# Plain attention's scores: from one product of three bf16 parts on 96 rows to two float32r parts on two row groups of 64

## The chip, the cores and the metric

One core of a Trainium2 chip runs the whole kernel. The metric is the device time of one execution in microseconds. TensorE (PE) multiplies matrices; its weight loads stand as PEld in the profile. VectorE is DVE, ScalarE is ACT, GpSimd is POOL, and SyncE (SP) issues all DMAs of the passes told of here, in order, on one queue.

## What is computed

128 images go through an embedding, a plain attention of 12 heads without an output projection, a causal attention, a mixture of 64 small experts and a final norm. The part that the change touches:

```
tokens = patches @ W_map.T + b_map + positions        # 197 tokens of 192 numbers
x      = layernorm(tokens) * ln_w + ln_b
q, k, v = per head of 16: x_h @ Wq.T + bq, ...        # 12 heads
att    = softmax(q @ k.T / sqrt(16))
tokens = tokens + att @ v                             # plain attention
```

The causal attention follows, with its own q, k and v.

## The kernel before

The program is a chain of passes, each over all 128 images: `embed_pass`, `attend_pass` (plain), `attend_pass` (causal), routing and experts, combination. In each pass every engine runs its own list of steps in order, written out by hand: step c works on several images at once, each in another phase (b2 = c - 2, b3 = c - 3 and so on), and semaphores order the engines. Four places in SBUF rotate (R = 4). Tokens are padded to 198 = 2 x 99.

**Embedding.** TensorE makes tokens, q, k and v in f32. ScalarE writes the high bf16 part of q and k (`split_high`, L310), VectorE the rest (`left_of`, L338), GpSimd the middle and the low part (L282, L284). SyncE stores the three parts in `scr["qk1"]` (L263): 96 partitions x 12 pieces of 396 bytes an image.

**Plain attention.** A score is a sum over 16 numbers of a head, each split in three bf16 parts; the six products of parts that count are stacked on 96 rows (`STACK`), so a score tile is one bf16 product over 96 rows, 99 columns of weights and 198 columns streamed. Each image's scores are made twice. First as *query scores* (L821, queries on partitions): VectorE takes each query's maximum (L770), TensorE turns the maxima (L925), ScalarE copies them negated (L721), GpSimd splits them in three parts (`max_parts`, L611 to L618), and SyncE writes these as three rows under the stack of q (L561), where rows of ones stand under k. Two images later they are made as *key scores* (L843, keys on partitions, 99 rows, maximum already taken off), and ScalarE takes the exponential (L713).

Step c has six slots k = 0 to 5. In each, TensorE first makes four key scores of image b4 (`key_scores`, L826; two PSUM buffers of two banks each, `sk`), then four query scores of image b2 as two fills f = 2k and 2k + 1 (`query_scores`, L808; two banks, `sq`: fill f waits until VectorE has taken the maxima of fill f - 2). After that come other products by slot:

- k = 0: transposes of image b6 (L916), then value products of b5 (L858)
- k = 1: the turned maxima of b3 (L925), which wait for VectorE's L775, then turned sums (L864)
- k = 2: q of the next attention for b6 (`turned_times`, L873, twelve float32r products), then value products
- k = 3: turned sums
- k = 4: k of the next attention (L873), then value products
- k = 5: v of the next attention (`tokens_times`, L881)

ScalarE's order in a step is the exponential of each slot, then in slot 0 the cast of the transposed image (L716), in slot 2 the high part of q (L179), in slot 5 the copy of v (L739), with copies of sums between. VectorE's order is the two maxima of each slot, then in slot 0 the low part of the cast (L775), in slots 1 and 3 the division by the sums (L791, L793), in slot 2 the rest of q (L784). SyncE's order in a step: six loads of q and k (L552), the three writes of maxima once GpSimd has made them (wait at L559), the load of tokens (L567), the stores (L578, L581).

Of the kernel before, what the change touches and what calls it, by code (L numbers as in the profile page):

```python
# [30 lines left out]
HEADS = 12  # L31
# [150 lines left out]
def embed_pass(nc, n, A, scr):  # L182
    R = 4
    DEPTH = 4
    with ExitStack() as ctx:
# [17 lines left out]
        rest = m.sb("e_rest", [CH, 2, 2, 2, SP])  # L203
        parts = m.sb("e_parts", [CH, R, 2, 2, PARTS, SP], BF16)
# [30 lines left out]
        middle = m.event("e_middle", 2)  # L235
        low = m.event("e_low", 2)
# [5 lines left out]
        def _(sp):  # L242
# [10 lines left out]
            def step(c):  # L253
# [4 lines left out]
                if b.inside(n):  # L258
                    sp.wait_ge(v_copied.sem, v_copied.at(b))
                    for rows in SHARES:  # L260
                        sp.dma_start(scr["tv1"][b.number, rows], tv[rows, b.place]).then_inc(stored.of(b), 16)
                    sp.wait_ge(low.sem, low.at(b))
                    sp.dma_start(scr["qk1"][b.number].rearrange("i c a p s -> p (i c a) s"),  # L263
                                 parts[:, b.place].rearrange("p i c a s -> p (i c a) s")).then_inc(stored.of(b), 16)
# [3 lines left out]

        @block.gpsimd
        def _(pool):  # L270
            for e in (middle, low):
                e.seed(pool)

            def step(c):
                b = c - 3
                u = b.parity
                if b.inside(n):
                    for i in range(2):
                        pool.wait_ge(left.sem, left.at(b, i + 1))
                        pool.wait_ge(stored.of(b - 4), stored.at(b - 4))  # L280
                        m.hold(pool)
                        pool.tensor_copy(parts[:, b.place, i, :, place_of(i, 1)], rest[:, u, i]).then_inc(middle.sem, 1)  # L282
                        pool.wait_ge(middle.sem, middle.at(b, i + 1))
                        pool.tensor_tensor(parts[:, b.place, i, :, place_of(i, 2)], rest[:, u, i], parts[:, b.place, i, :, place_of(i, 1)],  # L284
                                           ALU.subtract).then_inc(low.sem, 1)
            pipeline(pool, n, DEPTH, R, step)

        @block.scalar
        def _(act):
# [5 lines left out]
            def step(c):  # L295
# [11 lines left out]
                for i, (done, p) in enumerate(((q_done, qp), (k_done, kp))):  # L307
                    if b3.inside(n):
                        act.wait_ge(done.sem, done.at(b3))
                        split_high(nc.scalar, parts[:, b3.place, i, :, place_of(i, 0)], p[:], SCALES[i]).then_inc(high.sem, 1)  # L310
# [9 lines left out]
        def _(dve):  # L320
# [14 lines left out]
            def left_of(b3, i, p):  # L335
                dve.wait_ge(high.sem, high.at(b3, i + 1))
                dve.wait_ge(low.sem, low.at(b3 - 2, i + 1))
                nc.vector.scalar_tensor_tensor(out=rest[:, b3.parity, i], in0=p[:], scalar=SCALES[i],  # L338
# [89 lines left out]
def attend_pass(nc, n, A, scr, causal):  # L428
# [4 lines left out]
    with ExitStack() as ctx:  # L433
# [97 lines left out]
        def heads_of(fill):  # L531
            return fill // 6, 2 * (fill % 6)
# [266 lines left out]
        def _(pe):  # L799
# [84 lines left out]
            def step(c):  # L884
# [7 lines left out]
                for k in range(6):  # L892
# [5 lines left out]
                    if b4.inside(n):  # L898
                        key_scores(b4, k)
# [750 lines left out]
```

## Time and profile before

| | us |
|---|---|
| median of 3 runs | 4905.67 |
| lowest and highest | 4903.66, 4913.21 |
| the profiled execution | 4908.6 |
| its span (first to last instruction) | 4906.8 |

The page gives the busy time of each engine and the span in 40 slices. Plain attention lies between 905 and 2468 us of the span, embedding before it, causal attention from 2474 to 3856 us.

```profile
## 2 busy tenths in 40 slices
PE   8999999899999999999979999999999788889964
...
DVE  4555555566666666666556666666666599960057
ACT  3444444466666666666635555555555377764446
POOL 3444444466666666666656666666666488861135
PEclk9999999899999999999979999999999699999965
```

Each digit is a tenth of a slice of 122.7 us; slices 8 to 20 are plain attention. A busy TensorE is not one at its peak: the record of a product lasts from its start to its result, and products follow each other at shorter distances than their records are long, so distances between starts are what counts.

### The profile page before, as it was taken

The numbers are of one execution on the slowest core, as the hardware profiler recorded it, in microseconds if no ns is written. First come the engines' busy times: TensorE is split into PE (matmuls) and PEld (weight loads), VectorE is DVE, ScalarE is ACT, GpSimd is POOL, SyncE is SP. The second block draws the span as 40 slices with busy tenths as digits, with TensorE's granted clock in tenths as the row PEclk, the third lists the DMA queues.
The fourth block names the chain that finished last, engine by engine and source line by source line (L and its number), as shares of the span: only waits on it lengthen the run. The fifth ranks groups of instructions, "written<-read, shape, count | busy, mean of one in ns | idle before, by whom it ended". The sixth has DMA issues, their size and how long they took to land. (4 is left out here: it accounts for less than half of the span.)

```text
span 4906.8 us, 161306 instructions
## 1 busy us (share of the span) xinstructions
PE 4504.7 (92%) x48311; PEld 3888.5 (79%) x48311; DVE 3050.0 (62%) x8728; ACT 2746.9 (56%) x6788; POOL 2724.9 (56%) x4491
## 2 busy tenths in 40 slices
PE   8999999899999999999979999999999788889964
PEld 8999999688888888888867777777777566669953
DVE  4555555566666666666556666666666599960057
ACT  3444444466666666666635555555555377764446
POOL 3444444466666666666656666666666488861135
PEclk9999999899999999999979999999999699999965
DMA  6777777677777777777656665665666133339978
GB/s 172 202 201 201 202 202 203 145 168 168 168 164 169 167 166 167 168 167 164 149 122 131 134 132 131 132 134 130 130 135 132 56 94 92 93 104 276 276 237 255
DMA packets 697918, 789.88 MB, mean 161 GB/s; under 512 B 367345, under 2 KB 519887, under 8 KB 697840
## 3 DMA queue, kind: packets, MB, share of 16 engines
q1 hardware_dynamic: 697840, 788.92, 66.1%
q8 instruction: 40, 0.66, 0.1%
q14 instruction: 38, 0.31, 0.0%
HBM read 519.30 MB, written 265.72 MB: 160 GB/s over the span
## 5 line engine op out<-in xcount | busy, mean ns | idle before, releaser
L770 DVE TENSOR_REDUCE a_mx<-a_sq 99x2 f32<-99x394 f32 x1536 | 798.4, 561 | 377.2 <-PE a_sq L821 376.9
L770 DVE TENSOR_REDUCE c_mx<-c_sq 99x2 f32<-99x198 f32 (+1 forms) x1536 | 642.3, 459 | 315.0 <-PE c_sq L821 314.7
L713 ACT ACTIVATE a_ex<-a_sk 99x792 f32<-99x792 f32 (+1 forms) x768 | 638.8, 832 | 106.6 <-PE a_sk L843 56.6
L713 ACT ACTIVATE c_ex<-c_sk 99x792 f32<-99x792 f32 (+1 forms) x768 | 512.3, 667 | 247.1 <-PE c_sk L837 173.9
L379 PE MATMUL e_tokp<-e_wmap,e_ptT 128*99 128x192 f32 x3072 | 544.3, 327 | 20.8 <-DVE e_cvar L332 20.8
L634 POOL TENSOR_SCALAR_AFFINE_SELECT c_ex<-c_ex 99x396 f32<-99x396 f32 (+1 forms) x768 | 422.0, 550 | 232.2 <-ACT c_ex L713 228.1
L379 PEld LDWEIGHTS e_tokp<-e_wmap,e_ptT 128*99 128x99 f32 x3072 | 483.2, 167 | 21.3 <-issue 20.8
L821 PE MATMUL a_sq<-a_ks,a_qs 96*99 96x198 bf16 x3072 | 441.5, 255 | 31.3 <-DMA a_ks<-scr_qk 16.4
L282 POOL CAST e_parts<-e_rest 96x396 bf16<-96x396 f32 x256 | 176.8, 691 | 483.1 <-DVE e_rest L338 483.1
L821 PE MATMUL c_sq<-c_ks,c_qs 96*99 96x99 bf16 (+1 forms) x3072 | 417.7, 231 | 0.0
L843 PE MATMUL a_sk<-a_qs,a_ks 99*99 99x198 bf16 (+1 forms) x3072 | 408.5, 254 | 3.0 <-issue 2.2
L818 PE MATMUL c_sq<-c_maskb,c_identb 99*99 99x198 bf16 x1536 | 376.7, 262 | 21.3 <-DMA c_ks<-scr_qk 17.9
L843 PEld LDWEIGHTS a_sk<-a_qs,a_ks 99*99 99x99 bf16 (+1 forms) x3072 | 287.4, 126 | 124.6 <-issue 112.9
L821 PEld LDWEIGHTS a_sq<-a_ks,a_qs 96*99 96x99 bf16 x3072 | 293.2, 126 | 82.3 <-DVE a_mx L770 46.8
L858 PE MATMUL a_pvp<-a_ex,a_vx 99*32 99x198 f32 (+1 forms) x6144 | 337.9, 337 | 0.6 <-issue 0.5
L821 PEld LDWEIGHTS c_sq<-c_ks,c_qs 96*99 96x99 bf16 x3072 | 325.1, 128 | 0.0
L858 PE MATMUL c_pvp<-c_ex,c_vx 99*32 99x198 f32 (+1 forms) x6144 | 278.1, 299 | 27.5 <-issue 0.8
L698 ACT COPY c_ot<-c_pvp 128x198 f32<-128x198 f32 x384 | 124.7, 325 | 299.7 <-PE c_pvp L858 299.7
L858 PEld LDWEIGHTS c_pvp<-c_ex,c_vx 99*32 99x32 f32 (+1 forms) x6144 | 163.1, 110 | 131.8 <-DVE c_on L793 76.9
L284 POOL TENSOR_TENSOR e_parts<-e_rest,e_parts 96x396 bf16<-96x396 f32 x256 | 224.5, 877 | 20.5
L818 PEld LDWEIGHTS c_sq<-c_maskb,c_identb 99*99 99x99 bf16 x1536 | 194.5, 127 | 51.8 <-DVE c_mx L770 31.6
L843 PE MATMUL c_sk<-c_qs,c_ks 99*99 99x198 bf16 x1536 | 213.4, 261 | 9.6 <-issue 8.8
(196 smaller groups left out, 11487.7 us busy)
## 6 DMA issues: line engine op xcount, KB each, us to landing
e_ptT<-in_x SPq DMA_DIRECT2D x128, 594.0 KB
x_w<-in_fc SPq DMA_DIRECT2D x128, 576.0 KB, 5.8
scr_qk<-e_parts SPq DMA_DIRECT2D x128, 445.5 KB
scr_qk<-a_parts SPq DMA_DIRECT2D x128, 445.5 KB
scr_tv<-e_tv SPq DMA_DIRECT2D x128, 288.0 KB
a_tv<-scr_tv SPq DMA_DIRECT2D x128, 288.0 KB
scr_tv<-a_res SPq DMA_DIRECT2D x128, 288.0 KB
c_tv<-scr_tv SPq DMA_DIRECT2D x128, 288.0 KB
```

The lines of the kernel that those rows point to most:

```text
L282: pool.tensor_copy(parts[:, b.place, i, :, place_of(i, 1)], rest[:, u, i]).then_inc(middle.sem, 1)
L284: pool.tensor_tensor(parts[:, b.place, i, :, place_of(i, 2)], rest[:, u, i], parts[:, b.place, i, :, place_of(i, 1)], ALU.subtract).then_i ...
L379: mm = nc.tensor.matmul(tokp[b.parity][:, t], ptT[:, b.place, k, t * TT:(t + 1) * TT], wmap[:, k], start=(k == 0), stop=(k == KC - 1))
L634: pool.affine_select(block_of, block_of, pattern=[[0, G], [1, TT]], compare_op=ALU.is_ge, fill=0.0, base=0, channel_multiplier=-1).then_in ...
L698: nc.scalar.copy(ot[:, b.parity, g], pv).then_inc(o_copied.sem, 1)
L713: nc.scalar.activation(to, of, ACT.Exp).then_inc(exped.sem, 1)
L770: nc.vector.reduce_max(mx[:, b2.parity, qt, h:h + 2], sq[f % 2][:, :, 0:width], AX.X).then_inc(maxed.sem, 1)
L818: nc.tensor.matmul(bank[:, :, qt * TT:(qt + 1) * TT], identb[:], maskb[:].broadcast_to([TT, 2, TT]), start=True, stop=False, skip_group_ch ...
L821: mm = nc.tensor.matmul(bank[:, j, 0:keys], qs[0:STACK, b.place, h + j, qt * TT:(qt + 1) * TT], ks[0:STACK, b.place, h + j, 0:keys], start ...
L843: mm = nc.tensor.matmul(buf[0:rows, a, j * SP:(j + 1) * SP], ks[:, b.place, h, kt * TT:kt * TT + rows], qs[:, b.place, h, :], start=True, ...
L858: mm = nc.tensor.matmul(to, vx[0:rows, b.place, kt, G * g + j, :], of, start=(kt == 0), stop=(kt == 1), skip_group_check=causal)
```

## The change

- **Embedding** keeps two float32r parts of q and k (high and rest) instead of three bf16 parts. VectorE writes the rest straight into the parts; GpSimd has no work left in this pass. The store has 96 x 8 pieces of 792 bytes.
- **Layout in plain attention.** The three products of parts that count take 48 rows of f32r. Heads 0 to 5 stand on partitions 0 to 47, heads 6 to 11 on 64 to 111, and the maxima, now two parts, on the two rows after each. Loads are eight instead of six for an image (the same bytes, pieces of 4752 instead of 2376 bytes), writes of maxima four instead of three; GpSimd has two operations instead of four for them.
- **Scores.** `shared_scores` issues key scores of image b4 by turns with query scores of image b2; the order of the query fills is such that the two always lie on different row groups of 64. They are float32r products over 48 or 50 rows, 99 columns of weights, 198 streamed.
- **Start.** Rows of ones are set over 32 partitions by GpSimd (first in its list) and over 32 by VectorE, and SyncE's first load waits for both.
- The causal pass has its bf16 scores as before, and its parts are still three bf16 parts.

```diff
-        rest = m.sb("e_rest", [CH, 2, 2, 2, SP])
-        parts = m.sb("e_parts", [CH, R, 2, 2, PARTS, SP], BF16)
+        parts = m.sb("e_parts", [CH, R, 2, 2, 2, SP], F32R)
...
-                    sp.wait_ge(low.sem, low.at(b))
+                    sp.wait_ge(left.sem, left.at(b))
                     sp.dma_start(scr["qk1"][b.number].rearrange("i c a p s -> p (i c a) s"),
-                                 parts[:, b.place].rearrange("p i c a s -> p (i c a) s")).then_inc(stored.of(b), 16)
+                                 parts[:, b.place].rearrange("p i c a s -> p (i c a) s").bitcast(F32)).then_inc(stored.of(b), 16)
...
-        @block.gpsimd
-        def _(pool):
-            for e in (middle, low):
-                e.seed(pool)
-
...
-                if b.inside(n):
-                    for i in range(2):
-                        pool.wait_ge(left.sem, left.at(b, i + 1))
-                        pool.wait_ge(stored.of(b - 4), stored.at(b - 4))
-                        m.hold(pool)
-                        pool.tensor_copy(parts[:, b.place, i, :, place_of(i, 1)], rest[:, u, i]).then_inc(middle.sem, 1)
-                        pool.wait_ge(middle.sem, middle.at(b, i + 1))
-                        pool.tensor_tensor(parts[:, b.place, i, :, place_of(i, 2)], rest[:, u, i], parts[:, b.place, i, :, place_of(i, 1)],
-                                           ALU.subtract).then_inc(low.sem, 1)
-            pipeline(pool, n, DEPTH, R, step)
...
             def left_of(b3, i, p):
                 dve.wait_ge(high.sem, high.at(b3, i + 1))
-                dve.wait_ge(low.sem, low.at(b3 - 2, i + 1))
-                nc.vector.scalar_tensor_tensor(out=rest[:, b3.parity, i], in0=p[:], scalar=SCALES[i],
-                                               in1=parts[:, b3.place, i, :, place_of(i, 0)], op0=ALU.mult,
+                dve.wait_ge(stored.of(b3 - 4), stored.at(b3 - 4))
+                nc.vector.scalar_tensor_tensor(out=parts[:, b3.place, i, :, 1], in0=p[:], scalar=SCALES[i],
+                                               in1=parts[:, b3.place, i, :, 0].bitcast(F32), op0=ALU.mult,
                                                op1=ALU.subtract).then_inc(left.sem, 1)
...
-        qs = m.sb(X + "qs", [AUG, R, HEADS, SP], BF16)
-        ks = m.sb(X + "ks", [AUG, R, HEADS, SP], BF16)
+        if causal:
+            qs = m.sb(X + "qs", [AUG, R, HEADS, SP], BF16)
+            ks = m.sb(X + "ks", [AUG, R, HEADS, SP], BF16)
+        else:
+
+            qs = m.sb(X + "qs", [128, R, HC, SP], F32R)
+            ks = m.sb(X + "ks", [128, R, HC, SP], F32R)
...
-        mxp = m.sb(X + "mxp", [HEADS, 2, PARTS, SP], BF16)
+        mxp = m.sb(X + "mxp", [HEADS, 2, PARTS, SP], BF16) if causal else m.sb(X + "mxp", [HEADS, 2, 2, SP], F32R)
...
-        max_in_place = m.transfers(X + "max_in_place", 3)
+        max_in_place = m.transfers(X + "max_in_place", 3 if causal else 4)
...
+        def half(h):
+            return slice(64 * (h // HC), 64 * (h // HC) + 3 * DH), slice(64 * (h // HC), 64 * (h // HC) + 3 * DH + 2)
+            if not causal:
+
+                return ((0, 6), (1, 6), (0, 8), (1, 8), (0, 10), (0, 0), (1, 10), (1, 0), (0, 2), (1, 2), (0, 4), (1, 4))[fill]
...
+                    else:
+                        if b.is_number(0):
+                            sp.wait_ge(ks_ones, 1)
+                            sp.wait_ge(ks_ones_above, 1)
+                        for c2 in range(2):
+                            for stack, i, at, of in ((qs, 0, 0, slice(0, 1)), (qs, 0, DH, slice(0, 2)),
+                                                     (ks, 1, 0, slice(0, 2)), (ks, 1, 2 * DH, slice(0, 1))):
+                                at += 64 * c2
+                                sp.dma_start(stack[at:at + (of.stop - of.start) * DH, b.place].rearrange("r h s -> r (h s)").bitcast(F32),
+                                             qk_in[b.number, i, c2, of].rearrange("a (d h) s -> (a d) (h s)",
+                                                                                  d=DH)).then_inc(qk_in_place.of(b), 16)
                 if b.is_number(0):
                     sp.dma_start(w[:], A["wout" if causal else "wqkv2"].rearrange("(c p) d -> p c d", p=CH)).then_inc(weighed, 16)
...
+                    else:
+                        for a in range(2):
+                            for c2 in range(2):
+                                at = 64 * c2 + 3 * DH + a
+                                sp.dma_start(qs[at:at + 1, b.place].bitcast(F32),
+                                             mxp[c2 * HC:(c2 + 1) * HC, b.parity, a].bitcast(F32)).then_inc(max_in_place.of(b), 16)
                 b = c - 2
...
+            def ones_of_keys(of):
+                pool.memset(of, ONE_TWICE if causal else 1.0).then_inc(ks_ones, 1)
+                pool.wait_ge(ks_ones, 1)
+            if not causal:
+                ones_of_keys(ks[32:64].rearrange("p r h s -> p (r h s)").bitcast(F32))
...
+                if not causal:
+                    pool.tensor_tensor(low, of, high.bitcast(F32), ALU.subtract).then_inc(max_low.sem, 1)
+                    return
...
-                        act.wait_ge(max_rest.sem, max_rest.at(b3 - 2))
+                        if causal:
+                            act.wait_ge(max_rest.sem, max_rest.at(b3 - 2))
+                        else:
+                            act.wait_ge(max_low.sem, max_low.at(b3 - 2))
...
+            if not causal:
+                nc.vector.memset(ks[96:128].rearrange("p r h s -> p (r h s)").bitcast(F32), 1.0).then_inc(ks_ones_above, 1)
...
+            def shared_scores(b4, b2, k):
+
+                g, kt = k // 2, k % 2
+                rows = TT - kt
+                if b4.inside(n):
+                    bank_of_keys(b4, k)
+                for j in range(G):
+                    f = 2 * k + j // 2
+                    if b4.inside(n):
+                        h = G * g + j
+                        mm = nc.tensor.matmul(sk[k % 2][0:rows, j // 2, (j % 2) * SP:(j % 2 + 1) * SP],
+                                              ks[half(h)[1], b4.place, h % HC, kt * TT:kt * TT + rows],
+                                              qs[half(h)[1], b4.place, h % HC], start=True, stop=True)
+                        if j == G - 1:
+                            mm.then_inc(scored_k.sem, 1)
+                    if b2.inside(n):
+                        qt, h = heads_of(f)
+                        h += j % 2
+                        if j % 2 == 0:
+                            bank_of_queries(b2, f)
+                        mm = nc.tensor.matmul(sq[f % 2][:, j % 2], qs[half(h)[0], b2.place, h % HC, qt * TT:(qt + 1) * TT],
+                                              ks[half(h)[0], b2.place, h % HC], start=True, stop=True)
+                        if j % 2:
+                            mm.then_inc(scored_q.sem, 1)
...
-                    if b4.inside(n):
-                        key_scores(b4, k)
-                    if b2.inside(n):
-                        query_scores(b2, 2 * k)
-                        query_scores(b2, 2 * k + 1)
+                    if causal:
+                        if b4.inside(n):
+                            key_scores(b4, k)
+                        if b2.inside(n):
+                            query_scores(b2, 2 * k)
+                            query_scores(b2, 2 * k + 1)
+                    else:
+                        shared_scores(b4, b2, k)
...
-              "qk1": ([n, 2, 2, PARTS, CH, SP], BF16), "qk2": ([n, 2, 2, PARTS, CH, SP], BF16),
+              "qk1": ([n, 2, 2, 2, CH, SP], F32), "qk2": ([n, 2, 2, PARTS, CH, SP], BF16),
```

## Rows read from the trace of the kernel before

**Rows 1.** Windows: us; busy PE, PEld, DVE, ACT, POOL; PEclk, DMA, GB/s.

```profile
200.00:800.00 600.00, 600.00 (x4430) 596.32 (x4429) 321.10 (x710) 265.20 (x796) 272.90 (x355) 1.00 0.76 202
1200.00:2300.00 1100.00, 1090.81 (x13281) 916.70 (x13279) 756.21 (x1660) 732.36 (x1292) 674.11 (x1106) 1.00 0.74 167
```

**Rows 2.** Timeline, TensorE, one image of plain attention: start us, us, work, count.

```profile
1497.48 0.34 PE L881 MATMUL a_pvp<-a_wh,a_hTl 96*99 96x192 f32 x2
1497.65 0.51 PE L843 MATMUL a_sk<-a_qs,a_ks 99*99 99x198 bf16 x4
1498.00 0.51 PE L821 MATMUL a_sq<-a_ks,a_qs 96*99 96x198 bf16 x4
...
1501.61 0.41 PE L873 MATMUL a_work<-a_hTh,a_wh 96*96 96x198 f32 x2
...
1502.59 0.35 PE L873 MATMUL a_work<-a_hTl,a_wh 96*96 96x198 f32 x2
1502.87 0.88 PE L858 MATMUL a_pvp<-a_ex,a_vx 99*32 99x198 f32 x16
1503.68 0.55 PE L843 MATMUL a_sk<-a_qs,a_ks 99*98 99x198 bf16 x4
...
1505.70 0.41 PE L873 MATMUL a_work<-a_hTh,a_wh 96*96 96x198 f32 x2
...
1509.59 0.51 PE L843 MATMUL a_sk<-a_qs,a_ks 99*99 99x198 bf16 x4
```

**Rows 3.** Timeline, VectorE, the same image; x2 are two maxima.

```profile
1499.63 0.57 DVE L775 TENSOR_TENSOR a_hTl<-a_work,a_hTh 96x396 fp32r<-96x396 f32 x1 [0.21 <-ACT a_hTh L716]
1500.36 1.04 DVE L770 TENSOR_REDUCE a_mx<-a_sq 99x2 f32<-99x394 f32 x2 [0.16 <-PE a_sq L821]
...
1503.66 0.57 DVE L784 SCALAR_TENSOR_TENSOR a_rest<-a_work,a_parts 96x396 f32<-96x396 f32 x1 [0.77 <-ACT a_parts L179]
1504.44 1.04 DVE L770 TENSOR_REDUCE a_mx<-a_sq 99x2 f32<-99x394 f32 x2 [0.22 <-PE a_sq L821]
```

**Rows 4.** Timeline, last pass, half clock: products on partitions 0-63, 64-127 alternating.

```profile
4763.86 1.60 PE L1552 MATMUL o_zp<-o_yb,o_mix 64*99 64x192 f32 x8 [1.87 <-POOL o_yb L1482]
...
4763.97 0.93 PEld L1552 LDWEIGHTS o_zp<-o_yb,o_mix 64*99 64x99 f32 x6
```

**Rows 5.** Timeline, embedding, TensorE: f32 products on all rows.

```profile
400.79 2.12 PE L379 MATMUL e_tokp<-e_wmap,e_ptT 128*99 128x192 f32 x12
402.74 0.84 PE L409 MATMUL e_qp<-e_xT,e_wqkv 97*96 97x198 f32 x4
```

**Rows 6.** Timeline, routing pass, TensorE: from 99 rows to 64 rows.

```profile
4102.62 0.33 PE L1263 MATMUL r_cTp<-r_ident,r_cw 99*64 99x99 f32 x2
4102.88 0.38 PE L1266 MATMUL r_dTp<-r_ident,r_dw 64*99 64x64 f32 x2
```

**Rows 7.** Timeline, ScalarE, the same image of plain attention.

```profile
1497.85 0.48 ACT L739 COPY a_res<-a_pvp 99x384 f32<-99x384 f32 x1 [0.60 <-PE a_pvp L881]
1498.39 0.83 ACT L713 ACTIVATE a_ex<-a_sk 99x792 f32<-99x792 f32 x1
1499.12 0.48 ACT L716 CAST a_hTh<-a_work 96x396 fp32r<-96x396 f32 x1
```

**Rows 8.** Timeline, start of plain attention: SyncE's queue and GpSimd.

```profile
905.48 0.43 SPq L552 DMA_DIRECT2D a_qs<-scr_qk  x1
905.96 0.42 SPq L552 DMA_DIRECT2D a_ks<-scr_qk  x1
...
908.08 4.06 POOL L600 MEMSET a_ks<- 3x4752 f32 x1
```

**Rows 9.** Timeline, plain attention, SyncE's queue (SPq): DMA issues.

```profile
1501.07 0.32 SPq L552 DMA_DIRECT2D a_ks<-scr_qk  x1
1503.59 2.35 SPq L561 DMA_DIRECT2D a_qs<-a_mxp  x3
...
1509.88 1.38 SPq L552 DMA_DIRECT2D a_ks<-scr_qk  x1
```

## What the change will do to the time

> **What bounds the kernel now.** I read the windows first, for the share of each engine inside a pass; then the timelines of TensorE, ScalarE and VectorE for one image of plain attention, for the distances between starts; then the places elsewhere in the trace where two products run on two row groups; last SyncE's queue. In embedding TensorE is busy for all of 600 us, and GpSimd, whose work the change takes away there, for 273 [rows 1]: no other engine sets that pass. In plain attention TensorE is busy 1091 of 1100 us at granted clock 1.00, VectorE 756, ScalarE 732 [rows 1]. But "busy" hides who is late. One image takes 11.94 us: its slot 0 begins at 1497.65, the next one's at 1509.59 [rows 2]. In it TensorE waits twice for VectorE's maxima, before fill 5 and before fill 9: the maxima end at 1501.40 and 1505.48, and the float32r products behind these fills start 0.21 and 0.22 us later [rows 2, 3], which is just two score products. So the period is one loop in three parts:
>
> - A, from slot 0 (1497.65) to the q products (1501.61), 3.96 us: copy of v, exponential, cast (ScalarE), low part and two maxima (VectorE), fill 5.
> - B, to the k products (1505.70), 4.09 us: q products, high part, rest, two maxima, fill 9.
> - C, to the next slot 0, 3.89 us: TensorE alone.
>
> A faster score counts only where it shortens one of these.
>
> **Embedding.** It loses GpSimd's casts and subtractions, and its store gets 768 pieces of 792 bytes instead of 1152 of 396. TensorE's list is the same and is full [rows 1]: 0 us. The new wait of VectorE (L338, for the store of four images before) is one that ScalarE's high part in front of it already has; behind it on VectorE queue the reciprocal and the normalization, and TensorE's transposes wait for those. The store now waits for VectorE, earlier than for GpSimd. If TensorE stopped covering this pass, VectorE at 321 us of 600 is next, so nothing is lost there.
>
> **The scores.** An image has 48 score products of 0.088 us (four in 0.35 us [rows 2]), 4.2 us of TensorE. Afterwards they are 24 pairs. The price of a pair is nowhere in this pass, so I bound it. If both products run side by side, it is that of one float32r product of 198 columns: eleven distances from 1501.61 to 1502.69 (the second of the two at 1502.59), 0.093 us with the start [rows 2]. If one follows the other it is 0.175 (two bf16 distances) to 0.186 us. The nearest row is the last pass, where f32 products alternate between partitions 0-63 and 64-127: eight within 1.60 us, the last record 0.52 long, so eight starts in 1.08 us at half clock, that is about three intervals of 0.32 to 0.43 between pairs [rows 4]. One such product alone with the whole array takes 0.163 us at full clock (twelve in 1.95 us [rows 5]), 0.325 at half. A pair thus costs what one costs, weight loads included: six of these end within 0.93 us [rows 4]. I take 0.093 us.
>
> **Switching the array's division.** Going from 99 rows to 64 rows, the next product starts at 4102.88, where the distance of its predecessors (0.085) would give 4102.79: 0.09 us more [rows 6]. The value products on groups of columns show the same: 1502.87 instead of 1502.78 [rows 2]. Before, only value products switch, in and out, three times an image. Afterwards every change between scores and other products is a switch: nine more (in and out of slots 0 to 5, less those that value products already pay), 0.84 us of TensorE an image. TensorE's own account is then -4.2 + 2.2 + 0.8 = -1.2 us. Not all of it arrives, by the loop:
>
> - A. The copy of v starts 0.03 us after its products, now 0.11 after slot 0 begins instead of 0.20, for slot 0 starts one switch later. Then 0.54 to the exponential, 0.73 to the cast, 0.51 to the low part [rows 3, 7]. The key scores are there in time (3 x 0.093 + 0.25 + 0.04 = 0.57 before 0.65). The low part begins at 1.89; a maximum can follow 0.48 after it, as one does another (1.04 less 0.56 [rows 3]). Before, it came after 0.73, because fill 2 was late (the bracket "PE a_sq" in [rows 3]); fill 2 now comes about 0.3 us earlier. Two maxima of 1.04: 3.41. Then 0.21 - 0.175 + 0.186 + 0.09 for fill 5 and a switch: **3.72** instead of 3.96.
> - B. The rest of q starts 2.05 us after the q products [rows 2, 3], unchanged. The maxima follow after 0.48 instead of 0.78 (again they waited for TensorE), 1.04, and 0.32 for fill 9 and a switch: **3.89** instead of 4.09. Fill 6 must be done 2.53 us after the q products began: 1.26 to the value products, 0.81 through them [rows 2], 0.38 for the scores, 2.45. That is close; a dearer pair would show here.
> - C. Slot 5's eight scores shrink from 0.70 to 0.37, two switches add 0.18: **3.74** instead of 3.89.
>
> The sum is 11.35 us, 0.59 less than 11.94; 128 images give -75.5 us. What is late next is VectorE's and ScalarE's part of A and B.
>
> **The maxima's split.** GpSimd has two operations less, and the three writes become four; they land for a step that begins over 5 us later. Cover: that distance. Cost 0 while SyncE keeps up (below).
>
> **The start.** SyncE's first load was issued at 905.48, before the ones were set; the memset takes 4.06 us [rows 8], set by its length of 4752, which stays. Now the load waits for it: +3.7 us; and an image needs two more issues of 0.48 us [rows 8]: +1.0. All loads are queued behind this wait, and TensorE waits for them. Its bounds are 0 (a faster memset) and 6 us. I take +4.7.
>
> **Sum.** -75.5 + 4.7 = -70.8 us. Against the profiled execution, 4908.6 (1.8 over its span), that is 4837.8; the median of the runs is 2.9 lower, so 4835. About 0.2% (10 us) is what a measurement can tell from no change. The forecast's own range is 4800 to 4880: below, switches that cost half and gaps between engines that close further; above, pairs of 0.11 us (eight pairs lie on the loop) and SyncE just over the loop.
>
> **Rival 1, slower: the two products don't run side by side.** Then a pair costs 0.175 to 0.186 us and the switches are paid for nothing. Key scores would end 0.25 to 0.3 us later than the copy of v allows, and fills 5 and 9 and slot 5 have eight more pairs at +0.08 to +0.093: the loop is 12.26 to 12.39, +0.32 to +0.45 an image, and with the start 4951 to 4968. It decides from about 0.14 us a pair. Against it stand the pairs in [rows 4]; for it, that those were f32 at half clock, where a product is streamed long enough to hide any weight load: nothing shows two float32r weight loads of 99 columns within 0.093 us. Chance 0.17.
>
> The Trainium skill says in "TensorE: Matmul & The Clock Gate", section "Part 3: Packing small matmuls — row/col tiling", that weight loads overlap products in flight only where the row group differs. By that rule each group would load and multiply by turns, and the time would be this rival's. The pairs in [rows 4] follow each other at the pace of one product with loads between, so this trace speaks against it.
>
> **Rival 2: issue is the limit.** With 48 products in half the time TensorE's sequencer may not keep up. The densest stretch now is sixteen value products whose starts lie within 0.55 us (0.88 less a record of 0.33 [rows 2]), 0.037 us each; a pair needs 0.046 each. So it should hold. If it didn't, with a pair of 0.124, the loop would be 11.67 and the time 4876. Chance 0.06.
>
> The same page, section "Part 2: What happens when you issue a matmul", gives about 62 ns of microcode per product where hardware decoding is off. That would be this rival; the sixteen value products above are faster than it.
>
> **Rival 3: SyncE's queue becomes the loop.** SyncE waits from 1501.39 to 1503.59 for the split maxima [rows 9]: 2.2 of 11.94 us, so it is occupied for 9.74. Two more loads (0.48 each) and one more write (2.35 / 3 = 0.78) make 11.48, already over 11.35. Against: one load is stalled for 1.38 us instead of 0.43 behind the big store [rows 9], and with half as many pieces to queue this stall may go (10.5). For: if each of the first ones stalls so, it is 12.4. At 11.6 the time is 4867, and from 11.9 on nothing is gained. Chance 0.12.
>
> **Rival 4: the clock.** Plain attention has granted clock 1.00; the last pass, with long idle stretches, ran its row-group products at 0.50, the level of 1.2 GHz [rows 4]. If plain attention fell to that level, TensorE's part of the loop would double: over 500 us slower. TensorE stays busy most of the time, so 0.03. That the change leaves score time as it is for another reason: 0.02, near 4900 to 4940.
>
> **How the numbers follow.** Forecast 0.60, rivals 0.17, 0.06, 0.12, 0.03, 0.02. Faster by over 0.2%: the forecast, rival 2 and most of rival 3, 0.74; within 0.2%: 0.06; slower 0.20. The range reaches from 4800 into rival 1, to 4960.
>
> **What the profile will show.** Right: in plain attention a key score and a query score start under 0.02 us apart and pairs 0.09 to 0.10; about 0.09 extra at each change to other products; about 11.35 us an image; TensorE waits for VectorE longer than now before fills 5 and 9; embedding's length as before; the first load about 4 us later. Wrong: pairs at 0.14 or more (rival 1), SyncE without a wait at L559 (rival 3), a clock below 1.00 in that pass (rival 4), or an image over 11.7 us.

## The result, and the profile after

The changed kernel takes 5876.1 us (median of four, 5856.82 to 6111.58; the highest ran at a granted clock of 0.71 and is left out of the ratio). The kernel before, run beside it, takes 4909.44 (4903.66 to 4924.45). The ratio is 1.195, interval 1.189 to 1.202: nearly a fifth slower, where 4835 was forecast and 4800 to 4960 given as range. The profiled execution is 5856.82 us, its span 5854.7.

The page of the changed kernel, TensorE's busy share and granted clock in 40 slices:

```profile
PE   8999998999999999999999979999999978888975
PEclk9999995555555555555555579999999988999985
```

From the seventh slice to the 23rd the clock is at half; from the eighth on TensorE is busy for 90% of each slice or more. The windows of the changed kernel, with the columns of [rows 1]:

```profile
200.00:800.00 600.00, 600.00 (x4432) 596.33 (x4431) 272.67 (x710) 264.31 (x797) 0.00 (x0) 1.00 0.78 224
1200.00:2300.00 1100.00, 1100.00 (x8165) 812.64 (x8165) 480.92 (x1019) 458.09 (x794) 368.28 (x567) 0.50 0.44 103
3500.00:4500.00 1000.00, 909.68 (x12601) 756.87 (x12599) 656.96 (x1719) 531.45 (x1052) 614.39 (x1145) 1.00 0.61 132
```

Embedding's window is as full as before, with GpSimd at 0.00 [rows 1]; causal attention (the third row) runs at 1.00. Plain attention, from 901 to 3417 us instead of 905 to 2468, holds the whole loss: 2516 us for 1563. The granted clock falls at 897.65 us, in TensorE's wait for the pass's first loads, and stays at 0.50, the level of 1.2 GHz (1.00 is 2.4 GHz), for 2505 us. Before, it was there from 889.4 to 933.8 us only.

The timeline of TensorE in the changed kernel, one image at half clock; it answers to [rows 2]:

```profile
2001.33 0.48 PE L883 MATMUL a_sk<-a_qs,a_ks 50*99 50x198 f32 x1
2001.33 0.48 PE L893 MATMUL a_sq<-a_ks,a_qs 48*99 48x198 f32 x1
2001.61 0.37 PE L883 MATMUL a_sk<-a_qs,a_ks 50*99 50x198 f32 x1
2001.61 0.37 PE L893 MATMUL a_sq<-a_ks,a_qs 48*99 48x198 f32 x1
2001.78 0.37 PE L883 MATMUL a_sk<-a_qs,a_ks 50*99 50x198 f32 x1
2001.78 0.37 PE L893 MATMUL a_sq<-a_ks,a_qs 48*99 48x198 f32 x1
...
2020.74 0.48 PE L883 MATMUL a_sk<-a_qs,a_ks 50*99 50x198 f32 x1
```

A key score and a query score start together, and pairs follow each other by 0.17 us: 198 columns at 1.2 GHz are 0.165. So the change does what it says, and the pair has the price that the forecast gave it, at half the clock. Slot 0 comes again after 19.41 us instead of 11.94. TensorE sets this period alone: VectorE, which it waited for before [rows 2, 3], now waits for it:

```profile
2002.03 1.04 DVE L793 TENSOR_REDUCE a_mx<-a_sq 99x2 f32<-99x394 f32 x2 [2.12 <-PE a_sq L893]
2005.24 1.04 DVE L793 TENSOR_REDUCE a_mx<-a_sq 99x2 f32<-99x394 f32 x2 [0.98 <-PE a_sq L893]
```

The kernel before came out of its own half-clock start here (timeline, TensorE, kernel before):

```profile
914.52 1.04 PE L821 MATMUL a_sq<-a_ks,a_qs 96*99 96x198 bf16 x4 [0.33 <-DVE a_mx L770]
...
929.82 0.87 PE L843 MATMUL a_sk<-a_qs,a_ks 99*99 99x198 bf16 x4 [1.91 <-issue]
930.48 0.87 PE L821 MATMUL a_sq<-a_ks,a_qs 96*99 96x198 bf16 x4
931.14 0.87 PE L843 MATMUL a_sk<-a_qs,a_ks 99*98 99x198 bf16 x4
931.80 0.92 PE L821 MATMUL a_sq<-a_ks,a_qs 96*99 96x198 bf16 x4
```

Rounds (a round is what TensorE does in one step) of query scores alone, four at a time with gaps, did not raise it; the first scores of keys and queries without a gap, on 96 and 99 rows, did, at 933.8. These are the products that the change puts on 64 rows.

### The profile page after: what moved, and what is told of

It reads as the page before. It is cut to its first block and busy times, and to the rows that moved or that the text cites. A ratio compares the mean times of both kernels' runs of the same rounds, so it can differ in the third digit from the quotient of the medians.

```text
span 5854.7 us, 160403 instructions
## 1 busy us (share of the span) xinstructions
PE 5465.2 (93%) x48311; PEld 4447.1 (76%) x48311; DVE 3023.2 (52%) x8729; ACT 2761.3 (47%) x6788; POOL 2222.7 (38%) x3723
## 5 line engine op out<-in xcount | busy, mean ns | idle before, releaser
L883 PEld LDWEIGHTS a_sk<-a_qs,a_ks 50*99 50x99 f32 (+1 forms) x3072 | 566.0, 273 | 328.1 <-issue 292.0
L893 PE MATMUL a_sq<-a_ks,a_qs 48*99 48x198 f32 x3072 | 756.2, 397 | 23.5 <-DMA a_ks<-scr_qk 19.8
L883 PE MATMUL a_sk<-a_qs,a_ks 50*99 50x198 f32 (+1 forms) x3072 | 754.4, 395 | 1.1 <-issue 1.1
L908 PE MATMUL a_pvp<-a_ex,a_vx 99*32 99x198 f32 (+1 forms) x6144 | 595.0, 537 | 0.0
L893 PEld LDWEIGHTS a_sq<-a_ks,a_qs 48*99 48x99 f32 x3072 | 566.0, 273 | 28.3 <-issue 20.4
L626 POOL CAST a_mxp<-a_mxn 12x198 fp32r<-12x198 f32 x128 | 43.4, 339 | 977.4 <-ACT a_mxn L742 977.4
L848 PE MATMUL c_sq<-c_maskb,c_identb 99*99 99x198 bf16 x1536 | 377.1, 263 | 21.1 <-DMA c_ks<-scr_qk 17.6
L908 PEld LDWEIGHTS a_pvp<-a_ex,a_vx 99*32 99x32 f32 (+1 forms) x6144 | 228.5, 158 | 181.4 <-issue 78.4
L923 PE MATMUL a_work<-a_hTh,a_wh 96*96 96x198 f32 x1024 | 301.1, 396 | 3.1 <-DVE a_rest L807 1.9
L716 ACT COPY a_ot<-a_pvp 128x198 f32<-128x198 f32 x384 | 124.4, 324 | 376.8 <-PE a_pvp L908 376.8
L923 PE MATMUL a_work<-a_hTl,a_wh 96*96 96x198 f32 x1024 | 272.3, 367 | 0.0
```

Of the source, the lines that this page charges most:

```text
L626: pool.tensor_copy(high, of).then_inc(max_high.sem, 1)
L716: nc.scalar.copy(ot[:, b.parity, g], pv).then_inc(o_copied.sem, 1)
L848: nc.tensor.matmul(bank[:, :, qt * TT:(qt + 1) * TT], identb[:], maskb[:].broadcast_to([TT, 2, TT]), start=True, stop=False, skip_group_ch ...
L883: mm = nc.tensor.matmul(sk[k % 2][0:rows, j // 2, (j % 2) * SP:(j % 2 + 1) * SP], ks[half(h)[1], b4.place, h % HC, kt * TT:kt * TT + rows] ...
L893: mm = nc.tensor.matmul(sq[f % 2][:, j % 2], qs[half(h)[0], b2.place, h % HC, qt * TT:(qt + 1) * TT], ks[half(h)[0], b2.place, h % HC], st ...
L908: mm = nc.tensor.matmul(to, vx[0:rows, b.place, kt, G * g + j, :], of, start=(kt == 0), stop=(kt == 1), skip_group_check=causal)
```

## The experiments

Four theories stood at the start. H: the pass only starts at half clock, and once up the clock stays. P: pairs leave TensorE too little to stream. R: products that read a row group of 64, half the array, don't raise the clock (as it was put for the first run, they don't keep it up either). F: float32r scores as such, or another edit, keep it down. All runs but the last are one execution with a profile, beside one of the kernel before on the same chip (4904.18 for the first three runs told here; 4907.85 for those on one row group, on all rows, of the kernel before on 48 rows, and with products at the start of the pass; 4907.2 for the other four). Such single times of the kernel before spread from 4898 to 4925 us, so a difference of a few us between two runs shows nothing.

**Raise the clock once.** The added products, 24 of 512 columns on all 128 rows, stand ahead of the first value products of image 6 (`fill` is a tile of ones):

```
+                        if not causal and b6.is_number(0):
+                            for _ in range(24):
+                                nc.tensor.matmul(pvp[:], fill[:, 0:128], fill[:, 128:640], start=True, stop=True)
                         value_products(b5, 2)
```

> The changed kernel with 24 bf16 products of 512 columns on all 128 rows, written to a bank that is free, once at the seventh step of plain attention. Theory H (the pass only starts cold, because its first products are few; once the clock is up it stays): granted clock 1.00 from the burst on, 11.35 us an image, 4840 to 4860 us. Theory R (products on row groups of 64 don't keep the clock up): it rises with the burst and falls back within some tens of us, or doesn't rise; about 19.4 us an image, 5860 to 5890 us.

Measured: 4900.88 us, against 4904.18 for the kernel before. TensorE's timeline of this kernel, round the added products (L1005):

```profile
959.08 6.44 PE L1005 MATMUL a_pvp<-a_fill 128*128 128x512 bf16 x24
```

And the window of plain attention:

```profile
1200.00:2300.00 1100.00, 1083.07 (x13475) 820.74 (x13477) 755.52 (x1684) 750.26 (x1311) 611.33 (x936) 1.00 0.78 170
```

The first five follow each other by 0.427 us, those from the seventh on by 0.216; the clock is 1.00 from 961.3 to 2456 us, without a break, with no product added after them. So H is right as to staying up: the same rounds that ran at 0.50 for 2505 us keep 1.00, and the half of R that says that products on 64 rows can't keep the clock up falls. An image takes 11.76 us, not the 11.35 of the forecast. (The kernel before has such products in its routing pass, with a result that nobody reads.)

**One added product in each slot**, ahead of the scores, 512 columns on all 128 rows:

```
+                        if b4.inside(n) and b2.inside(n):
+                            bank_of_keys(b4, k)
+                            nc.tensor.matmul(sk[k % 2][:, 0, 0:512], fill[:, 0:TT], fill[:, 128:640], start=True, stop=True)
                         shared_scores(b4, b2, k)
```

> The changed kernel with one bf16 product of 512 columns on all 128 rows ahead of the scores in each of the six slots of every step of plain attention; it is overwritten by the key scores. Theories H and R: the clock rises to 1.00 and stays; 12.2 to 12.6 us an image (11.35, plus the part of 6 x 0.22 and three switches that lies on the loop), 4940 to 5000 us. If neither holds (the clock is down for another reason than what TensorE does): 0.50 throughout, about 22 us an image, 6190 us.

Measured: 5313.91 us. The image takes 22.47 us at 0.50 until 1617.6 us; there the clock rises, and to the pass's end it is 1.00, with an image of 12.94 us. Neither forecast held. Six such products, apart from each other, raise it late, after some 30 images that look alike; why in that one stays open. Once up it held here too.

**Alternation undone**: four key scores, then four query scores in each slot.

```
                 for j in range(G):
                     if b4.inside(n):
                         ... key score
+                for j in range(G):
                     if b2.inside(n):
                         ... query score
```

> The changed kernel with the alternation undone: in each slot four key scores, then four query scores, on the same row groups and with the same data, so that no two products run side by side except where the groups change. Theory R: the clock stays at 0.50, because half the rows work at a time; about 19.4 + 24 x 0.167 = 23.4 us an image, 6370 us. A theory P (it is the pairs: 24 instead of 48 stretches of streaming leave TensorE with too little work) expects clock 1.00, about 12.4 us an image and 4965 us.

Measured: 5857.77 us, clock 0.50 throughout, image 19.47 us against 19.41. TensorE's timeline of this kernel:

```profile
2001.89 0.48 PE L882 MATMUL a_sk<-a_qs,a_ks 50*99 50x198 f32 x1
2001.90 0.48 PE L894 MATMUL a_sq<-a_ks,a_qs 48*99 48x198 f32 x1
```

The list holds four products of one kind and then four of the other, and yet they run side by side, the later ones taken forward onto the idle row group. So this run, which was meant to tell P from R, could not. The order by turns is worth 0.06 us an image, and it has no part in the clock.

**P against R: all scores on one row group**, so one after the other (heads 6 to 11 read the rows of heads 0 to 5):

```
         def half(h):
-            return slice(64 * (h // HC), 64 * (h // HC) + 3 * DH), slice(64 * (h // HC), 64 * (h // HC) + 3 * DH + 2)
+            return slice(0, 3 * DH), slice(0, 3 * DH + 2)
```

> Changes the computation: all twelve heads read rows 0-49 (heads 0 to 5 twice), so every score product runs on the one row group 0-63 and the products follow one another; their count, type, columns and rows are as in the changed kernel. Question: why does the granted clock stay at 0.50 in plain attention. Theory P (pairs: two products at a time leave too little streaming): the serial scores stream twice as long, as before the change, so the clock rises soon after the pass's start and stays up; image 12.2 to 12.5 us (48 products at 0.093 and the switches), 4940 to 4980 us. Theory R (products on 64 rows, half the array, don't raise the clock, however long they stream): 0.50 through the pass; 24 more products of 0.167 us at half clock, image about 23.4 us, 6350 to 6400 us.

Measured: 6402.26 us; image 23.41 us. The window of plain attention in this kernel:

```profile
1200.00:2300.00 1100.00, 1100.00 (x6772) 861.69 (x6768) 429.35 (x846) 382.38 (x658) 306.71 (x470) 0.50 0.37 85
```

The scores stream as long as before the change, one after the other, TensorE is busy for all of 1100 us, and the clock is 0.50. P falls: without pairs it stays down as well.

**F against R: the same float32r scores on the whole row range**, `half` giving rows 0 to 111 (0 to 113 with the maxima, which are multiplied by zero), with zeros in the unused rows:

```
-            return slice(64 * (h // HC), 64 * (h // HC) + 3 * DH), slice(64 * (h // HC), 64 * (h // HC) + 3 * DH + 2)
+            return slice(0, 112), slice(0, 114)
```

> Changes the computation: each score product reads rows 0-111 (key scores 0-113), that is two heads at once, and the maxima are multiplied by zero; so float32r scores on the whole row range, one after the other, with no row groups and no switches around them. Theory R: the clock rises within some tens of us, as in the kernel before; 48 products of 0.093 us against 0.088 before, image 11.9 to 12.2 us, 4905 to 4945 us (the second memset at the start adds up to 4). Theory P gives the same. Theory F (float32r scores as such, or another edit, keep it down): 0.50 through the pass, over 6000 us.

Measured: 4938.99 us. The clock rises at 943.7, 6 us after key scores and query scores begin to come close behind each other, and stays. Window and two scores from this kernel's views:

```profile
1200.00:2300.00 1100.00, 1100.00 (x12976) 952.37 (x12974) 736.36 (x1622) 721.35 (x1262) 590.39 (x900) 1.00 0.77 164
```

```profile
1501.32 0.26 PE L886 MATMUL a_sk<-a_qs,a_ks 114*98 114x198 f32 x1
1501.41 0.26 PE L896 MATMUL a_sq<-a_ks,a_qs 112*99 112x198 f32 x1
```

F falls: float32r scores of the same columns and count do raise the clock when they read 112 rows. They follow each other at 0.09 to 0.10 us, and the image is 12.21.

**R without the change: the kernel before, its scores cut to rows 0 to 47**, in bf16, one after the other, nothing else touched:

```
-                    mm = nc.tensor.matmul(bank[:, j, 0:keys], qs[0:STACK, b.place, h + j, qt * TT:(qt + 1) * TT],
-                                          ks[0:STACK, b.place, h + j, 0:keys], start=not causal, stop=True,
+                    mm = nc.tensor.matmul(bank[:, j, 0:keys], qs[0:STACK if causal else 48, b.place, h + j, qt * TT:(qt + 1) * TT],
+                                          ks[0:STACK if causal else 48, b.place, h + j, 0:keys], start=not causal, stop=True,
...
-                                                  ks[:, b.place, h, kt * TT:kt * TT + rows], qs[:, b.place, h, :],
+                                                  ks[0:AUG if causal else 48, b.place, h, kt * TT:kt * TT + rows], qs[0:AUG if causal else 48, b.place, h, :],
```

> The kernel before the change, with its bf16 score products cut to rows 0-47, so the sums over the other rows and the maxima are left out of the scores; all else as before. Serial, bf16, one row group. Theory R: the clock stays at 0.50 in plain attention although nothing else of the change is there; image 23 us or more, over 6200 us. Theories P and F: the clock rises at about 930 to 960 us as before; nine more switches an image, 4905 to 5010 us.

Measured: 6281.47 us. The kernel before, with nothing of the change but fewer rows, stays at 0.50 from 890 us to the end of the pass, with an image of 22.81 us; its window:

```profile
1200.00:2300.00 1100.00, 1100.00 (x6949) 833.07 (x6948) 412.47 (x866) 397.45 (x675) 356.26 (x580) 0.50 0.39 87
```

**R at the rise itself: the 24 products on 64 rows.** One change to the first run:

```
-                                nc.tensor.matmul(pvp[:], fill[:, 0:128], fill[:, 128:640], start=True, stop=True)
+                                nc.tensor.matmul(pvp[:], fill[0:64, 0:128], fill[0:64, 128:640], start=True, stop=True)
```

> The run with 24 products of 512 columns in image 6, with one thing changed: the 24 products read 64 rows instead of 128; they are as many, as long and as dense. Theory R (products on 64 rows don't raise the clock): it stays at 0.50 in and after them, and the pass runs as in the changed kernel, plus at most 24 x 0.427 = 10 us: 5860 to 5875 us. If any dense stream raises it: about 4901 us, as with 128 rows.

Measured: 5869.29 us. TensorE's timeline and two windows of this kernel, to be read beside the first run's:

```profile
957.37 10.42 PE L1005 MATMUL a_pvp<-a_fill 64*128 64x512 bf16 x24
```

```profile
957.00:967.80 10.80, 10.80 (x31) 3.57 (x33) 0.78 (x2) 0.80 (x2) 0.00 (x0) 0.50 0.37 71
1200.00:2300.00 1100.00, 1100.00 (x8163) 813.13 (x8162) 482.89 (x1024) 459.17 (x794) 370.66 (x568) 0.50 0.45 103
```

As many products, of as many columns, as dense; 128 rows raise the clock 2.2 us after their start, 64 rows don't in 10.4.

**What holds it: one row group, with the 24 products on 128 rows** (the edits of the first run and of the run on one group together).

> Changes the computation: all heads read rows 0-49, so all score products are on one row group, one after the other, and 24 products of 512 columns on 128 rows stand in image 6 to raise the clock. Question: what holds it once it is up. If only the rise needs the whole array and any busy TensorE holds it, it stays at 1.00: image 12.2 of the run on all rows plus nine switches of 0.09 to 0.17 us, 13.0 to 13.8 us, 5060 to 5160 us. If serial 64-row products also lose it, while pairs side by side kept it in the run with pairs: back to 0.50 after the 24 products, image 23.4, 6380 to 6410 us.

Measured: 5134.27 us, clock 1.00 from 968.1 to 2661 us; image 13.35. The window:

```profile
1200.00:2300.00 1100.00, 1100.00 (x11863) 888.93 (x11864) 678.77 (x1484) 658.97 (x1154) 538.15 (x824) 1.00 0.72 149
```

To hold the clock asks less than to raise it: the rounds with serial scores on 64 rows, which could not raise it, keep it. The first run, with pairs, has 11.76 us an image and this one 13.35, so at full clock pairs are worth 1.6 us against the same products one after the other.

**Raise it at the start of the pass**: 40 of these products as TensorE's first work there, while it waits for the loads.

```
+            if not causal:
+                pe.wait_ge(fill_ready, 1)
+                for _ in range(40):
+                    nc.tensor.matmul(pvp[:], fill[:, 0:128], fill[:, 128:640], start=True, stop=True)
             pe.wait_ge(const, n_const)
```

> The changed kernel with 40 products of 512 columns on all 128 rows, of ones, that TensorE does first thing in the pass, into a bank that isn't used yet, while it waits for the first loads (901 to 913 us); nothing else is changed. Theory H (only the cold start is the fault; up once, the clock stays): it rises in these products, stays up from the first image, and the pass loses the 60 us at half clock that the run with 24 products in image 6 had: 4860 to 4885 us. If the thin first images let it fall again, it stays at 0.50 to the end: 5860.

Measured: 5850.0 us. The windows of this kernel show the rise and the fall:

```profile
901.00:904.00 3.00, 2.55 (x7) 0.92 (x8) 1.96 (x2) 0.00 (x0) 3.00 (x1) 0.50 0.07 22
905.00:914.00 9.00, 7.12 (x35) 3.23 (x34) 1.36 (x1) 0.00 (x0) 2.85 (x2) 1.00 0.71 146
915.00:931.00 16.00, 12.80 (x46) 8.45 (x45) 12.78 (x24) 1.61 (x2) 1.44 (x3) 0.50 0.73 128
935.00:950.00 15.00, 14.67 (x132) 9.16 (x131) 8.22 (x17) 7.42 (x14) 2.31 (x5) 0.50 0.55 106
```

It rises at 904.7 and falls at 915.0: the products end at 911.9, TensorE then waits 1.9 us, and the first images have query scores only, four at a time with waits for VectorE between. From 935 on TensorE is busy again, and nothing raises it. So H lacked a condition: a clock raised ahead of these first rounds was lost in them.

**Fewer products**: 8 instead of 24 in image 6.

> The changed kernel with 8 products of 512 columns on 128 rows in image 6 instead of 24. With 24 the granted clock was up from the sixth on. Theory H/R: eight raise it too and save 16 x 0.216 = 3.5 us: 4894 to 4900 us. If the rise needs the whole stretch, it stays or falls back: 5860.

Measured: 4896.97 us against 4907.2; up at 959.6.

**Two places**: 10 products at the start of image 4's round, 8 in image 6's.

> Ten products of 512 columns on 128 rows at the start of image 4's round, where TensorE waits about 1.3 us for the maxima to land, and eight in image 6's. If the clock comes up at 934 to 936 us instead of 961 and the rounds of images 4 and 5 keep it: two rounds of 11.4 and 13 us become 9.5, less 2 us for the products: 4885 to 4893 us. If these thin rounds let it fall, the eight raise it again: 4896 to 4902.

Measured: 4901.47 us. Up at 936.8, down at 940.2, up again at 964.1: the round of image 4 did not keep it either, though TensorE was busy for 2.98 of these 3.42 us. What let the clock fall there was not tried further, and of the ten products no gain is seen.

**The kernel with 8 products, timed in five rounds.**

> The kernel with 8 products in image 6 once more, timed against the kernel before in five rounds, for an interval. By its image of 11.73 us against 11.93 over 122 images (-24 us), and a slower start (rounds of 11.4 and 15.6 us where the kernel before had 9.1 and 9.8: +8 us, and 4.7 for the loads that wait, of which embedding's earlier end gives some back): 4895 to 4900 against 4905 to 4909, ratio 0.997 to 0.999. If the clock's rise hangs on chance, some executions are near 5860.

Measured: 4892.59 us (median of 9, 4891.11 to 4897.82) against 4908.6 (4898.45 to 4918.41): ratio 0.9972, interval 0.9962 to 0.9983. No execution missed the rise, and this version is faster than the kernel before, by 0.3%. The traces give the change only a part of that. Plain attention is 1557.1 us in it, 1562.6 in the kernel before, 5.5 us less. From one product of turned maxima to the next, an image has 11.76 us instead of 11.93, which over 124 images is -21.1; the two rounds ahead of these, here still at half clock and the second with the 8 products in it, have 11.43 and 16.24 us where there were 9.10 and 9.77, +8.8; the start, with the later loads, takes 5.4 us longer and the end 1.4. Embedding is 3.7 us shorter, and causal attention, which the change doesn't touch, 5.4; in the traces of this case that pass has any length from 1371.7 to 1385.1.

## Why the prediction was wrong, step by step

**The step that failed is rival 4.** It named the right event, with a lower bound of its size (over 500 us; it was 947.9 of span, as TensorE at half clock sets the whole loop of 19.41 us), and gave it 0.03, on the ground that TensorE stays busy most of the time. That ground is wrong twice. Busy is not what tells: at 0.50 TensorE was busy 1100 of 1100 us, more than the 1091 at 1.00 [rows 1]. And the mean over the pass says nothing of its beginning. [rows 1] showed that the pass held 1.00; what had raised it, at 933.8 us, the prediction never looked at, though the profile showed the half-clock start of 44.4 us, and there it would have seen that the products that raised it are those that the change halves in rows. In its place the runs showed that the pass starts at 0.50, that scores on 64 rows don't raise the clock from there (nor do 24 dense products on 64 rows), and that one stretch of products on 128 rows ahead of full rounds does. [rows 4] was read for the pairs' distance alone; that these row-group products ran at half clock was put down to the idle stretches of that pass. Whether the products on 64 rows had a part in it there, no run here shows.

The Trainium skill, "TensorE: Matmul & The Clock Gate", section "Part 1: The HAM clock gate (the "warmup" mystery)", lets the gate go by how busy TensorE has been. For the rise, these traces agree only where the scores read 96 rows or more, or where products on 128 rows were added: with scores on 64 rows alone TensorE was busy for 1100 of 1100 us and the clock stayed at 0.50. By that rule rival 4 would have had no chance.

**Rival 1, pairs one after the other: fell.** The pair costs one product, 0.17 us at half clock and 0.09 to 0.10 at full. The rule of the Trainium skill, "TensorE: Matmul & The Clock Gate", section "Part 3: Packing small matmuls — row/col tiling", that a weight load overlaps products in flight only where the row group differs, does not agree with the run on all rows: products of 112 and 114 rows, each with its own weights, follow each other at 0.09 to 0.10 us, where 198 columns at 2.4 GHz are 0.083, and weight loads fill 952 of that window's 1100 us beside them.

**Rival 2, issue: fell.** Two products in 0.09 us are issued without a gap.

**Rival 3, SyncE's queue: fell.** In the run with 24 products SyncE still waits 0.69 us for the split maxima (its load ends at 1509.74, the write starts at 1510.43) and 0.74 ahead of the loads.

**The loop, with the clock up.** Here the forecast's mechanism can be judged, and its size was off too: 11.76 us an image is over the 11.7 that it named as a sign of being wrong. In the timed kernel the means over 110 images are A 3.84, B 4.03, C 3.90 us, where 3.72, 3.89 and 3.74 were forecast and 3.96, 4.09 and 3.89 stood before. The mis-sized term is the switch. TensorE, ScalarE and VectorE in the run with 24 products, one image (three views):

```profile
1505.68 0.33 PE L886 MATMUL a_sk<-a_qs,a_ks 50*99 50x198 f32 x1
...
1509.60 0.42 PE L926 MATMUL a_work<-a_hTh,a_wh 96*96 96x198 f32 x2
...
1513.63 0.43 PE L926 MATMUL a_work<-a_hTh,a_wh 96*96 96x198 f32 x2
...
1515.73 0.33 PE L886 MATMUL a_sk<-a_qs,a_ks 50*98 50x198 f32 x1
...
1515.90 0.26 PE L886 MATMUL a_sk<-a_qs,a_ks 50*98 50x198 f32 x1
...
1515.99 0.25 PE L886 MATMUL a_sk<-a_qs,a_ks 50*98 50x198 f32 x1
...
1516.09 0.25 PE L886 MATMUL a_sk<-a_qs,a_ks 50*98 50x198 f32 x1
...
1516.28 0.42 PE L934 MATMUL a_pvp<-a_wh,a_hTh 96*99 96x192 f32 x2
1516.54 0.34 PE L934 MATMUL a_pvp<-a_wl,a_hTh 96*99 96x192 f32 x2
...
1517.53 0.33 PE L886 MATMUL a_sk<-a_qs,a_ks 50*99 50x198 f32 x1
```

```profile
1506.44 0.83 ACT L733 ACTIVATE a_ex<-a_sk 99x792 f32<-99x792 f32 x1 [0.17 <-PE a_sk L886]
```

```profile
1508.16 1.03 DVE L796 TENSOR_REDUCE a_mx<-a_sq 99x2 f32<-99x394 f32 x2
```

Pairs of one slot start 0.09 to 0.10 us apart, but the second starts 0.17 after the first. The first product after the slot starts 0.19 after the last pair, and the two of 1516.28 take 0.42 where the two after them take 0.34. So a switch costs 0.09 us ahead of the first product, as the prediction read it from [rows 6], and about 0.08 more behind it. [rows 6] held a part of that too, unread: the two products of 64 columns take 0.38 us, those of 99 columns before them 0.33. The two runs whose TensorE is full at 1.00 price it by themselves: an image with 48 serial scores takes 13.35 us where these are on 64 rows and 12.21 where they are on 112; by the reckoning of the prediction the two differ by nine switches, 0.13 us each. On the loop it counts thus: in A the key scores of slot 0 end later and the exponential follows them, not the copy of v; before fills 5 and 9 the products start 0.41 us after the maxima end (1509.60 less 1509.19) instead of 0.31; in C the products of v and the way into slot 0 each pay.

**Embedding at 0, the start at +4.7: nearly right.** Embedding lasts 879.9 us in both traces that have the old one and 874.7 to 878.8 in the twelve that have the new one, so it gave 1 to 5 us where nothing was forecast; TensorE is as full as before, and no run tells where they come from. The first load now follows the pass's first instruction on SyncE by 4.70 us (905.56 less 900.86) instead of 0.43: 4.27 more, where 3.7 was priced for the wait for the ones. That this is near the +4.7 of the whole start is chance: TensorE's first score comes 12.00 us after that instruction instead of 8.27, 3.73 more.

## What to carry to other kernels

Before cutting a product to 64 rows, look in the trace for the stretch that raised TensorE's clock, and ask which of its products would read half the rows afterwards; a pass that starts after a wait may otherwise stay at half clock to its end, with a TensorE that looks full. Where pairs on two row groups pay, a few products over all 128 rows (here eight) brought the clock up, and pairs kept it; ahead of the thin first rounds it was lost again. Price a change of the array's division at both products behind it, not only at the distance to the first.

## What the runs showed of the hardware

- In these kernels the clock's rise went by the rows that products read, not by TensorE's busy time: 0.50 at 1100 of 1100 us busy with scores on 48 to 50 rows in bf16 or float32r, single or in pairs; up at 933.8 and 943.7 us with 96 to 114 rows. In the kernels that stayed at 0.50, too, products on 96 to 128 rows stood between the scores, twelve in a row among them, and did not raise it. The columns of weights were not varied. What the chip counts, and why the run with one product a slot rose at 1617.6 us and not before, stays open.
- Rise and hold are not alike: rounds with scores on one row group of 64, which did not raise the clock in 3022 us of plain attention at 0.50, kept it at 1.00 for 1693 us.
- TensorE takes a later product forward onto an idle row group: four key scores followed by four query scores in the list ran in pairs, 0.01 us apart.
